# The last layer norm ahead of the projections moved from VectorE to ScalarE in five attentions

## The reference

```python
def _layernorm(x, axis=-1, eps=1e-05):
    m = jnp.mean(x, axis=axis, keepdims=True)
    v = jnp.var(x, axis=axis, keepdims=True)
    return (x - m) / jnp.sqrt(v + eps)
...
    x = x + _L0_xattn_ref(_layernorm(x, axis=-1), ctx_512, ctx_512, ...)
    x = x + _L0_ffn_ref(_layernorm(x, axis=-1), ...)
    x = x + _L1_xattn_ref(_layernorm(x, axis=-1), ctx_512, ...)
    x = x + _L1_ffn_ref(_layernorm(x, axis=-1), ...)
    x = x + _L2_xattn_ref(_layernorm(x, axis=-1), ctx_512, ...)
    x = x + _L2_ffn_ref(_layernorm(x, axis=-1), ...)
    x = x + _L3_xattn_ref(_layernorm(x, axis=-1), ctx_512, ...)
    x = x + _L3_ffn_ref(_layernorm(x, axis=-1), ...)
```

## Time and profile before

| what | value |
|---|---|
| median of 3 runs | 2857.39 us (2856.14 to 2863.58) |
| profiled execution | 2860.57 us, span of the trace 2858.7 us |
| PE busy | 2194.7 us (77%) |
| DVE busy | 1834.4 us (64%) |
| ACT busy | 1319.3 us (46%) |
| POOL busy | 1209.8 us (42%) |
| mean granted TensorE clock | 0.872 of full |

### The profile page before, as it was taken

One profiled execution on the slowest core, in us unless ns is written; L12 is line 12 of the kernel. 1 busy time (PEld: TensorE's weight loads), 2 busy tenths in 40 slices (PEclk: granted clock), 3 DMA queues, 4 the chain that ended last, 5 costly groups with the idle time before them and its releaser, 6 DMA issues. The chain is left out here.

```text
span 2858.7 us, 68713 instructions
## 1 busy us (share of the span) xinstructions
PE 2194.7 (77%) x22450; PEld 1675.2 (59%) x22450; DVE 1834.4 (64%) x5129; ACT 1319.3 (46%) x2753; POOL 1209.8 (42%) x1900
## 2 busy tenths in 40 slices
PE   3846995999967368499999944998557999978533
PEld 2636994666645267377777733666344888866321
DVE  4945554666669455488888654776554666658686
ACT  2423552334334246254555443444434888854243
POOL 3544634555434444477777422331241333324211
PEclk9967997999979579699999967999666999989755
DMA  6021210000000223100000000000001111110001
GB/s 260 20 99 50 76 51 25 13 14 12 6 5 0 74 61 87 55 12 10 10 9 9 2 8 18 1 0 2 8 1 36 62 55 62 55 32 1 13 1 30
DMA packets 81044, 96.28 MB, mean 34 GB/s; under 512 B 16354, under 2 KB 60268, under 8 KB 78764
## 3 DMA queue, kind: packets, MB, share of 16 engines
q1 hardware_dynamic: 72628, 76.73, 8.3%
q0 software_dynamic: 8192, 16.79, 2.0%
HBM read 56.12 MB, written 37.36 MB: 33 GB/s over the span
## 5 line engine op out<-in xcount | busy, mean ns | idle before, releaser
L1852 DVE TENSOR_TENSOR l2f_experts_h_lo<-l2f_experts_h,l2f_experts_h_hi 128x512 fp32r<-128x512 f32 x256 | 182.2, 733 | 144.1 <-ACT l2f_experts_h_hi L1776 144.0
L889 POOL TENSOR_TENSOR a_pm<-a_pt,tri_post 128x256 f32<-128x256 f32 x256 | 179.7, 731 | 94.1 <-ACT a_pt L549 94.0
L1791 ACT ACTIVATE l2f_experts_h<-l2f_experts_f,l2f_experts_bias 128x512 f32<-128x512 f32 x256 | 174.9, 688 | 56.1 <-DVE l2f_experts_h_lo L1852 49.9
L684 DVE TENSOR_REDUCE l1s_negm<-l1s_s 128x3 bf16<-128x384 f32 x256 | 131.3, 557 | 108.3 <-PE l1s_s L386 106.8
L684 DVE TENSOR_REDUCE a_negm<-a_s 128x2 bf16<-128x512 f32 x256 | 164.6, 685 | 32.4 <-PE a_s L386 31.1
L1888 POOL TENSOR_TENSOR l2f_acc<-l2f_experts_tmp,l2f_acc 128x512 f32<-128x512 f32 x64 | 83.1, 1299 | 232.9 <-DVE l2f_experts_tmp L1822 232.9
L549 ACT ACTIVATE l1s_pt<-l1s_st 128x768 f32<-128x768 f32 x128 | 96.9, 812 | 160.3 <-PE l1s_st L421 160.3
L1776 ACT ACTIVATE l2f_experts_h_hi<-l2f_experts_h 128x512 fp32r<-128x512 f32 x256 | 154.4, 632 | 0.0
L549 ACT ACTIVATE a_pt<-a_st 128x1024 f32<-128x1024 f32 x128 | 126.3, 1061 | 3.1 <-PE a_st L421 3.1
L565 ACT ACTIVATE a_q_hi<-a_pa 128x256 fp32r<-128x256 f32 x64 | 24.7, 385 | 190.8 <-PE a_pa L352 190.8
L1711 PE MATMUL l2f_experts_f<-l2f_x_hi,l2f_experts_w_hi 128*128 128x512 f32 x256 | 100.8, 394 | 10.6 <-POOL l2f_experts_w_lo L1878 10.6
(11 more groups left out here) (551 smaller groups left out, 6993.9 us busy)
## 6 DMA issues: line engine op xcount, KB each, us to landing
expert_rows<-zeros SPq DMA_DIRECT2D x16, 1056.0 KB, 17.1
l2f_experts_wrow<-weights_by_expert SPq DMA_DIRECT2D x64, 256.0 KB
l0f_w<-in_l0f_w SPq DMA_DIRECT2D x8, 640.0 KB, 9.8
l0f_x_in_sb<-expert_rows SPq DMA_DIRECT2D x72, 64.0 KB
expert_rows<-l0f_y SPq DMA_DIRECT2D x72, 64.0 KB, 1.6
l1f_x_in_sb<-expert_rows SPq DMA_DIRECT2D x72, 64.0 KB
expert_rows<-l1f_y SPq DMA_DIRECT2D x72, 64.0 KB
l2f_experts_raw<-in_l2f_w SPq DMA_DIRECT2D x8, 512.0 KB
```

The costliest lines, as they stand in the source:

```text
L684: dve.tensor_reduce(dst, src, AX.X, ALU.max, negate=True).then_inc(max_done, 1)
L889: last = pool.tensor_tensor(pm[:, par, heads_, kt, :], pt[:, par, heads_, kt * (T + P):kt * (T + P) + P], K["tri_post"][:].unsqueeze(1).br ...
L1791: act.activation(h[:, j], psum_f[j][:], ACT.Gelu, bias=col(e, j)).then_inc(h_ready, 1)
L1852: dve.tensor_tensor(h_lo[:, pos % 2, j], h[:, j], h_hi[:, pos % 2, j].bitcast(F32), ALU.subtract)\
```

## The change

In the five attentions of `attention_rows` the last norm ahead of `turn` is no longer applied by VectorE as (x - mean) * rstd. GpSimd works out nm = -mean and shift_x = nm * rstd, and ScalarE applies rstd * x + shift_x at the end of its iteration, for the same unit as before (n+3 with U of 1). `rstd`, `nm` and `shift_x` keep one buffer each, so GpSimd waits, ahead of the next `rstds`, until ScalarE has read them, and VectorE's statistics wait for `shift_ready`.

```diff
+        nm, shift_x = sb("nm", [P, TT]), sb("shift_x", [P, TT])
+        nm_ready, shift_ready = sem("nm_ready"), sem("shift_ready")
...
+            def norm(b):
+                act.wait_ge(shift_ready, b + 1)
+                wait(act, xn_turned, b)
+                act.sem_inc(K["passed"], 1)
+                src = (x if NLN == 1 else residual)[:, bass.ds(b * TT, TT), :]
+                for t in range(TT):
+                    last = act.activation(xn[:, t, :], src[:, t, :], ACT.Identity, bias=shift_x[:, t:t + 1],
+                                          scale=rstd[:, NLN - 1, t:t + 1])
+                last.then_inc(xn_ready, 1)
...
+                na, ba, ua, posa = at(LEAD - plan[-1][0])
+                if inside(na) and ua == 0:
+                    norm(ba)
...
+                if i == NLN - 1:
+                    wait(dve, shift_ready, b)
                 dve.sem_inc(K["passed"], 1)
                 for t in range(TT):
                     last = dve.bn_aggr(mv[:, i, t, :], st6[:, i, t, :])
...
-                            ln_stats(ba, i) if what == "stats" else ln_apply(ba, i)
+                        elif what == "stats":
+                            ln_stats(ba, i)
+                        elif what == "apply" and i < NLN - 1:
+                            ln_apply(ba, i)
...
             def rstds(b, i):
                 pool.wait_ge(stats[i], b + 1)
+                if i == NLN - 1:
+                    wait(pool, xn_ready, b)
                 pool.sem_inc(K["passed"], 1)
                 pool.tensor_scalar(veps[:, i, :], mv[:, i, :, 1], EPS, None, ALU.add).then_inc(veps_ready[i], 1)
+                if i == NLN - 1:
+                    pool.tensor_scalar(nm[:], mv[:, i, :, 0], -1.0, None, ALU.mult).then_inc(nm_ready, 1)
                 pool.wait_ge(veps_ready[i], b + 1)
                 pool.tensor_tensor(rstd[:, i, :], veps[:, i, :], K["half"][:, 0:TT], ALU.pow).then_inc(rstd_ready[i], 1)
+                if i == NLN - 1:
+                    pool.wait_ge(rstd_ready[i], b + 1)
+                    pool.wait_ge(nm_ready, b + 1)
+                    pool.sem_inc(K["passed"], 1)
+                    pool.tensor_tensor(shift_x[:], nm[:], rstd[:, i, :], ALU.mult).then_inc(shift_ready, 1)
```

More of the change, by code:

```diff
@@ L651, in ln_stats @@
                     dve.wait_ge(merged, 2 * TT * (b + 1))
+                if i == NLN - 1:
+                    dve.sem_inc(K["passed"], 1)
+                    wait(dve, stats[i], b)
                 dve.sem_inc(K["passed"], 1)
@@ L664, in ln_apply @@
                 src = (x if i == 0 else residual)[:, bass.ds(b * TT, TT), :]
[L665 to L668, removed]
+                dst = residual[:, bass.ds(b * TT, TT), :]
                 for t in range(TT):
@@ L671, in ln_apply @@
                                              ALU.subtract, ALU.mult)
-                last.then_inc(xn_ready if final else scaled[i], 1)
+                last.then_inc(scaled[i], 1)
             def maxima(n, pos, i):
@@ L769, in emit @@
                             merge_choice(ba, (posa // U) % 2, i)
-                        elif what != "gather":
-                            ln_stats(ba, i) if what == "stats" else ln_apply(ba, i)
+                        elif what == "stats":
+                            ln_stats(ba, i)
+                        elif what == "apply" and i < NLN - 1:
+                            ln_apply(ba, i)
                 if inside(nw) and uw == U - 1 and store_t is None:
```

## The result

The changed kernel took 3067.4 us (median of 4 runs, 3061.8 to 3073.4), the kernel before 2859.7 us (median of 4, 2856.1 to 2863.6) in the same comparison. The ratio is 1.073, with a 95% interval from 1.070 to 1.075. The profiled execution of the changed kernel took 3064.9 us, its span is 3063.2 us, and the mean granted clock fell to 0.846. The forecast was 3063.

The account below looks back on a forecast made before the run. VectorE and TensorE near full, in a ring of engines with hardly any slack. 2860.57 + 103 (ring) + 3 (starts) + 17.5 (`l1s`, `a1`) = 2984, 2981 at the median, + 82 (clock) = 3063 us; range 2955 to 3135.

Parts of the forecast that it names:

- The ring: U=1 attentions: GpSimd's wait for ScalarE's norm delays `keys`, then `scores`; 9.9 us an iteration in `l0`, 103 us in all.
- Each sign that the prediction named: `l0`: `k_f` to `k_f` 10 us or more, late `kb_hi`, clock under 1.00, VectorE idle 2 us; `a1` transposes wait for `v_f`.
- the starts: Start of each U=1 attention: a later first norm, about 1 us each, 3 us.
- The clock: U=1 attentions: TensorE's gap before `scores` lowers its clock in each iteration; 1.95 us in 42 iterations, 82 us.
- `l1s`: Attention `l1s`: GpSimd's added 0.5 us delays `kb_hi` and so TensorE, 15 times; 7.5 us, bounds 0 and 12.
- `a1`: Attention `a1`: ScalarE's norm delays `v_f`, and 0.64 us reaches a full TensorE 16 times; 10 us, bounds 0 and 12.5.
- The clock holds: Rival, U=1 attentions: TensorE stays at full clock despite the gaps; 2981 us, chance 0.2.
- The clock stays at half all through: Rival, U=1 attentions: TensorE at half clock throughout, 3.9 us an iteration; 3145 us, chance 0.08.
- The wait is partly hidden: Rival, U=1 attentions: norm comes earlier against `keys`, half the 7.35 us left, clock does not fall; 2930 us, chance 0.12.
- Faster, VectorE sets the pace: Rival: `kb_hi` not late, three attentions save 0.65 us in some 12 iterations each; 2834 us, chance 0.03.

Follow-up runs that it names:

- e4: Kernel before, norm still on VectorE, plus one GpSimd wait ahead of `rstds` for ScalarE's last copy in the U=1 attentions: 2960.7 us, ratio 1.034.
- e1: Changed kernel with two buffers for the last norm's rstd and shift, so GpSimd waits for the norm before the last one: 2911.4 us, ratio 1.017.
- e2: Changed kernel with GpSimd running `preset` and `keys` ahead of `rstds` in the U=1 attentions, one buffer and the wait kept: 2909.5 us, ratio 1.017.
- e5: Changed kernel with ten unused 512-column matmuls filling TensorE's gap between transposes and `scores` in the U=1 attentions: 3006.5 us, ratio 1.051.
- e10: e8 with `a1`'s norm back on VectorE: 2853.2 us, ratio 0.999 against the kernel before.
- e6: Kernel before with only the three U=1 attentions changed, ScalarE's norm ahead of the copies, `l1s` and `a1` as before: 2855.7 us, ratio 0.998.
- e8: e3 with the product `shift_x` in `l1s` moved on GpSimd behind the gather and `keys`: 2857.3 us, ratio 0.999 against the kernel before.
- e9: Changed kernel with the edits of e1 and e2 together, the norm still behind the copies: 2901.3 us, ratio 1.016 against the kernel before.
- e3: Changed kernel with ScalarE's norm ahead of the copies in the U=1 attentions, one buffer and the wait kept: 2878.9 us, ratio 1.006.

## Why the prediction was right

**The ring.** Each sign that the prediction named is there: `l_veps` released by ACT `l_xn`, `scores` waiting for POOL `l_kb_hi`, VectorE idle before the maxima. That it is the wait together with what stands behind it is shown from both sides: e4 adds the wait alone and loses 99 us; e1 takes only the wait away, e2 only what stands behind it, and both win back over 155 us with all the added work still there. In these attentions the added work costs in the main where it stands in a ring. I had priced the ring at 103 us and 3 for the starts. At full clock it measured about 109 (115 less 5.6 of e5's own work). In the middle of the stages an iteration of e5 takes 9.96 us in `l0`, 10.14 in `l1c` and 9.00 in `l3`, against 7.05, 7.62 and 7.00 before: 2.9, 2.5 and 2.0 more, where I had 2.9, 2.2 and 2.25. The sum is 7.4 us for my 7.35, too small in `l1c` and too large in `l3`; fourteen times 7.4 are 104, and the other 5 lie at the first and last iterations. The recorded 7.0 and 7.71 were single iterations of before, whose lengths go in turn.

**The clock.** It falls after the gap, as said, and filling the gap lifts it. I had taken the middle between nothing and half clock all through, 1.95 us an iteration, 82 us. It measured some 72 us by the traces (66 and the 5.6 of e5's own work), 1.7 us an iteration. The middle was a choice, not a measurement, and it was some 10 us too much. With both gaps, some 4 us together, it fell in each iteration seen; with the 1.21 us alone, in e1, in three of the steady iterations of `l0`, while the others kept the full clock.

**`l1s`.** Mechanism right, size wrong: 16.3 us for 7.5. TensorE waits for `kb_hi`, as said (1.42 us in the row above). The term took the added work of 0.5 us; the rows have 0.92 us of delay in front of the gather, since the product also waits for its factor and leaves a larger gap before the gather. My upper bound of 12 was broken too.

**`a1`.** The transposes do wait for `v_f`, as said. But it cost 1.9 us and not 10: the wait was right, and that all of it is lost was wrong. Grouped lines of TensorE over 300 us of `a1` (busy time, mean ns, idle time before and its releaser) show a wait that came and one that went. The first is of the changed kernel, and this row has no idle time before the change; the second is of before, and has none after it:

```profile
L342 PE MATMUL a_pa<-ident,a_xn 128*128 128x128 f32 x22 | 4.8, 298 | 5.7 <-ACT a_v_f L603 5.7
```

```profile
L421 PE MATMUL a_st<-ident_bf,a_negm 128*128 128x128 bf16 x704 | 46.7, 219 | 3.4 <-DVE a_negm L684 2.5
```

For 11 samples the new wait is 5.7 us, 0.52 a sample and so 8.3 for 16, near the priced 0.64 and 10 (by its own terms 0.78 less 0.12, so 0.66). But 3.4 us of idle time before other matmuls, most of it for VectorE's maxima, is gone. VectorE no longer does the norm there; in e10, where it does again, 2.4 us of that idle time are back. The net is 2.3 us for 11 samples, 3.3 for 16, near the 1.9 of the stage and the 2 to 3 of e10. I had overlooked that VectorE's relief is worth something where TensorE now and then waits for it.

**The sum.** The ring was 6 us too small, `l1s` 9 too small, the starts and ends of stages 2 too small (5.3 of the span's growth for my 3), the clock 10 too large, `a1` 8 too large. The errors nearly cancel, and the median landed 4 us from the forecast. The mechanisms are shown; that the sum is so near is luck.

**The rivals.** *The clock holds* is what e5 makes true, and its 2981 would have been some 3001 (3006.5 less e5's own 5.6). *The clock stays at half all through* fell, since the clock comes back within the dense stretch: 1.03 us for the `scores_t` of each short iteration, and a mean clock of 0.76 to 0.79 in the three stages. *The wait is partly hidden* fell: ScalarE's order held in each iteration seen. *Faster, VectorE sets the pace*, needed `kb_hi` early; e6 and e8 give it that, and they come 4 to 6 us under the kernel before, not the 23 that 0.65 us an iteration would make, since VectorE's own `l_on_t` takes up a good part of it. I had not seen the second ring, through the norm's place on ScalarE: it was covered by the first, and e1, e2 and e9 lose some 27 to 33 us more than e3. By the profiles e9's U=1 attentions are 24.2 us longer than e3's, 9.3 in `l0`, 8.8 in `l3` and 6.1 in `l1c`.

What stays open: why the gap between the product and the gather on GpSimd is 0.57 us. The profile names ScalarE's `k_f` as the releaser in four of the eleven such gaps in `l1s`, and none in the other seven of the same length, so `k_f` isn't it; the gather has no need of it either. Open too is what slows VectorE's `l_on_t` in e6.

## What to carry to other kernels

When an edit puts a wait on an engine, write down what stands behind the waiting instruction in that engine's order and who waits for that, and follow the chain until it closes; if it closes within an iteration, its length is the new pace, whatever the busy shares say. Then cure by order before buffers: here moving two instructions ahead of the copies won back 190 of 208 us, while a second buffer alone left 50 and the buffer together with a new order on GpSimd 44. And where TensorE's new gaps recur in each iteration, price the clock with them, apart from the gaps.

## What the runs showed of the hardware

- With idle gaps of 1.2 and 2.8 us around two transposes in each iteration of 11.5 to 12.7 us, TensorE ran at 1.2 GHz behind them: window clock 0.50, sixteen value matmuls 1.94 us and not 1.07. With ten matmuls of no use in the larger gap the clock of the same stretch was 1.00 and the kernel was 61 us faster. So idle time of TensorE cost something here even where it had to wait anyway. With a gap of 1.21 us alone (e1) most iterations kept the full clock, and three in `l0` fell to half of it and took 8.8 to 9.1 us and not 7.46.
- VectorE's pair of 128x128 products `l_on_t` took 0.49 us in the changed kernel with GpSimd idle, 0.91 before and 1.12 to 1.21 in e6 with GpSimd at work beside it. The cause isn't shown.
- On GpSimd, operations on 128x2 elements take 0.22 us (scalar), 0.20 (product) and 0.72 (power), and the product of 0.20 us delayed the indirect DMA behind it by 0.77 us.
